# Folding two layer norms into the weights of a gated cross-attention block, with one norm chain and a reordered prologue

## The reference

```
# block 0: gated attention over the context, then RMS norm
memory_proj = context @ W_mem.T                     # (4, 512, 256)
attn        = softmax(x @ memory_proj.T / sqrt(256))
mc          = attn @ memory_proj
gate        = sigmoid(concat(x, mc) @ W_gate.T + b_gate)
fused       = x + gate * mc
x1          = fused * rsqrt(mean(fused^2) + 1e-6) * norm_w
# block 1: masked cross attention with 16 heads of 64, then a feed-forward part
q   = (layernorm(x1) * g_q + b_q) @ Wq / 8;  k, v = split(context @ Wkv)
x2  = x1 + tanh(attn_gate) * (softmax(where(mask, q @ k.T, -inf)) @ v) @ Wo
h   = gelu((layernorm(x2) * g_ff + b_ff) @ W1) @ W2
out = x2 + tanh(ff_gate) * h
```

## Time and profile before

| what | value |
|---|---|
| median of 3 executions | 231.49 us (231.4 to 231.99) |
| the profiled execution's own time | 232.58 us |
| its span, first to last instruction | 230.7 us |
| busy: PE, DVE, ACT, POOL | 212.7, 141.8, 127.4, 79.5 us |
| chain that ended last: PE, issue, DVE, POOL, ACT | 56%, 13%, 11%, 10%, 9% |

### The profile page before, as it was taken

One profiled execution on the slowest core, in us unless ns is written; L12 is line 12 of the kernel. 1 busy time (PEld: TensorE's weight loads), 2 busy tenths in 40 slices (PEclk: granted clock), 3 DMA queues, 4 the chain that ended last, 5 costly groups with the idle time before them and its releaser, 6 DMA issues.

```text
span 230.7 us, 4263 instructions
## 1 busy us (share of the span) xinstructions
PE 212.7 (92%) x1520; PEld 170.0 (74%) x1520; DVE 141.8 (61%) x296; ACT 127.4 (55%) x414; POOL 79.5 (34%) x82
## 2 busy tenths in 40 slices
PE   7769997998999999999999977999989999999994
PEld 4546544766976978976989855778867788998993
DVE  1575997635885556985655887867875567125410
ACT  3365754747457646567636466575449775028600
POOL 2030143943175333266331447636373007000000
PEclk9999997999999999999999999999999999999999
DMA  6984005050000000000000000050000000110011
GB/s 203 351 300 149 0 0 182 3 185 0 0 3 0 3 1 1 3 1 0 3 0 4 0 0 0 3 182 0 3 1 3 1 0 4 47 45 0 4 47 53
DMA packets 8463, 10.30 MB, mean 45 GB/s; under 512 B 754, under 2 KB 7668, under 8 KB 8052
## 3 DMA queue, kind: packets, MB, share of 16 engines
q1 hardware_dynamic: 7908, 9.71, 12.3%
q10 hardware_dynamic: 528, 0.26, 0.4%
HBM read 8.92 MB, written 1.05 MB: 43 GB/s over the span
## 4 chain that ended last, share of the span: by engine, by line
PE 56%; issue 13%; DVE 11%; POOL 10%; ACT 9%; POOLq 0%; ACTq 0%; DVEq 0%
PE bank L379 33%; ACT expd L585 6%; POOL probs L481 5%; PE bank L1080 4%; PE bank L1171 4%; PE bank L1050 3%; PE bank L1027 3%; PE bank L1090 3%; DVE neg_max L784 2%; PE bank L1229 2%; POOL wo_pair L519 1%; DVE probsT L797 1%; PE bank L1116 1%; PE bank L1134 1%; PE bank L1126 1%
## 5 line engine op out<-in xcount | busy, mean ns | idle before, releaser
L585 ACT ACTIVATE expd<-bank,neg_max 128x128 f32<-128x128 f32 (+1 forms) x136 | 50.5, 396 | 38.1 <-DVE neg_max L784 38.0
L481 POOL TENSOR_TENSOR probs<-expd,row_rcp 128x512 f32<-128x512 f32 x40 | 42.3, 1069 | 69.8 <-DVE row_rcp L792 63.2
L784 DVE TENSOR_REDUCE neg_max<-bank 128x4 f32<-128x512 f32 (+1 forms) x40 | 25.7, 683 | 6.0 <-PE bank L1050 3.6
L585 ACT ACTIVATION_READ_ACCUMULATOR expd<-bank,neg_max 128x1 f32 x136 | 29.3, 216 | 0.0
L379 PE MATMUL bank<-xhT_pair,wq_pair 128*128 128x256 f32 x192 | 27.5, 293 | 1.1 <-DVE fused L806 1.1
L379 PEld LDWEIGHTS bank<-xhT_pair,wq_pair 128*128 128x128 f32 x192 | 24.6, 194 | 5.0 <-DVE fused L806 1.9
L379 PE MATMUL bank<-wo_pair,oT_pair 128*128 128x256 f32 x192 | 26.6, 288 | 0.0
L1080 PE MATMUL bank<-ident,probs 128*128 128x128 f32 x160 | 22.6, 277 | 3.7 <-POOL probs L481 3.5
L379 PEld LDWEIGHTS bank<-wo_pair,oT_pair 128*128 128x128 f32 x192 | 23.6, 189 | 1.8
L1080 PEld LDWEIGHTS bank<-ident,probs 128*128 128x128 f32 x160 | 17.7, 140 | 8.4 <-POOL probs L481 7.1
L379 PE MATMUL bank<-wq_pair,gelu_pair 128*128 128x256 f32 x192 | 23.2, 281 | 0.4 <-issue 0.3
(11 more groups left out here) (125 smaller groups left out, 346.9 us busy)
## 6 DMA issues: line engine op xcount, KB each, us to landing
stage<-in_L_xattn_W_dram SPq DMA_DIRECT2D x2, 1024.0 KB, 5.0
x_sb<-in_x_dram SPq DMA_DIRECT2D x4, 256.0 KB, 8.7
wkv_sb<-in_L_xattn_Wkv_dram SPq DMA_DIRECT2D x1, 1024.0 KB, 9.2
stage<-in_L_xattn_Wq_dram SPq DMA_DIRECT2D x1, 1024.0 KB, 10.3
stage<-in_L_xattn_Wo_dram SPq DMA_DIRECT2D x1, 1024.0 KB, 5.4
out_dram<-x_sb SPq DMA_DIRECT2D x8, 128.0 KB, 1.7
ctx_sb<-in_ctx_dram SPq DMA_DIRECT2D x1, 768.0 KB, 7.1
probs<-in_L_xattn_W_gate_dram SPq DMA_DIRECT2D x1, 512.0 KB, 5.2
```

Source lines behind the costliest of these rows:

```text
L481: nc.gpsimd.tensor_tensor(probs[:, r, :].rearrange("p (h k) -> p h k", h=hb), expd[:, r, :].rearrange("p (h k) -> p h k", h=hb), row_rcp[: ...
L585: last = nc.scalar.activation(expd[:, r, h * w:(h + 1) * w], SC[n % 2][:, h * w:(h + 1) * w], ACT.Exp, bias=neg_max[:, r, h:h + 1], accum_ ...
L784: nc.vector.tensor_reduce(neg_max[:, r, 0:hb], SC[n % 2][:, :].rearrange("p (h k) -> p h k", h=hb), AX_X, ALU.max, negate=True).then_inc(d ...
```

## The change

- Both layer norms' scales are multiplied into Wq and W1 where these are split (a scale for each partition, since partition p holds rows 2p and 2p + 1). The offsets become biases of the queries and of the feed-forward part: `q_bias` and `f_bias`, 8 columns each, from 16 one-column float32 matmuls each (stages "qbias" and "fbias"). The query bias is added as queries are read from PSUM, the other one inside the Gelu. POOL's multiply and add on the normed tiles are gone.
- The chain of two norms becomes one. "rms" on DVE multiplies `fused` by the norm weight, takes statistics of that, then makes the mean square and var + epsilon x mean square; one power on POOL gives both roots. xhat comes from the product not yet scaled. POOL scales x_sb by the RMS root afterwards (in "xhat"). The stages "x1" and "ln1" are gone, and "xhat" stands where "x1" stood.
- A bank of keys is copied whole, odd ones by ACT and even ones by DVE.
- The prologue's order is new. Four broadcast rows of 128 KB are replaced by four loads of 2 values for each partition.

The diff, cut to its core (left out: allocations, semaphores, renamed views):

```diff
-    ("k", "hot", 0), ("splitq", 0), ("k", "hot", 3), ("gate", 0), ("k", "hot", 1), ("fuse", 0), ("rms", 0),
-    ("k", "hot", 2), ("k", "hot", 4), ("xT", 1), ("x1", 0), ("ln1", 0), ("k", "hot", 6), ("xhat", 0), ("k", "hot", 5),
-    ("y", 1), ("splitq", 1), ("k", "hot", 7), ("scores", "ctx", 1, 0), ("v", "hot", 0, 0), ("flag",), ("tiles",),
-    ("v", "hot", 1, 0), ("xhT", 0), ("v", "hot", 0, 1), ("norm", "ctx", 1, 0), ("exp", "ctx", 1, 0), ("q", 0, 0),
-    ("splito", 0), ("splito", 1), ("v", "hot", 1, 1),
+    ("k", "hot", 0), ("splitq", 0), ("k", "hot", 1), ("gate", 0), ("qbias",), ("k", "hot", 2), ("fuse", 0), ("rms", 0),
+    ("splitq", 1), ("k", "hot", 3), ("k", "hot", 4), ("xT", 1), ("xhat", 0), ("k", "hot", 5), ("tiles",),
+    ("y", 1), ("k", "hot", 6), ("xhT", 0), ("flag",), ("k", "hot", 7), ("scores", "ctx", 1, 0), ("q", 0, 0),
+    ("v", "hot", 0, 0), ("exp", "ctx", 1, 0), ("v", "hot", 0, 1), ("norm", "ctx", 1, 0),
+    ("splito", 0), ("splito", 1), ("v", "hot", 1, 0), ("v", "hot", 1, 1),
...
-    ((("x1", 1),), (("ln1", 1), ("q", 0, 3), ("xT", 2)), (("xhat", 1),)),
+    ((("xhat", 1),), (("q", 0, 3), ("xT", 2)), ()),
...
-    ((), (("gate", 1),), (("rms", 1), ("fuse", 1))),
-    ((("x1", 1),), (("q", 0, 3), ("ln1", 1)), (("xhat", 1),)),
+    ((), (("gate", 1),), (("rms", 1), ("fuse", 1), ("fbias", 0))),
+    ((("xhat", 1),), (("q", 0, 3),), ()),
...
-                    "xhT": [(dve["xhT"], c)], "k": [(dve["k"], c), (act["k"], c)],
+                    "xhT": [(dve["xhT"], c)], "k": [(act["k"], (c + 1) // 2)] if c % 2 else [(dve["k"], c // 2)],
...
+            for i, v in enumerate((lnq_g, lnq_b)):
+                load(lnq_cols[:, i, :], v.rearrange("(p k) -> p k", k=K), w_in["lnq"])
...
-            for i, v in enumerate((lnq_g, lnq_b, lnf_g, lnf_b)):
-                load(ln_rows[:, i, :], v.rearrange("(a d) -> a d", a=1).to_broadcast([P, D]), w_in["ln"])
+            for i, v in enumerate((lnf_g, lnf_b)):
+                load(lnf_cols[:, i, :], v.rearrange("(p k) -> p k", k=K), w_in["ln"])
...
+            sp.wait_ge(pe["qbias"], 1)
...
+            sp.wait_ge(pe["fbias"], 1)
...
-                        gp.wait_ge(dve["ms"], c)
-                        if c > 1:
-                            gp.wait_ge(dve["ve"], c - 1)
-                        nc.gpsimd.tensor_tensor(rms_r[:, :], ms[:, :], half_pow[:, :], ALU.pow
-                                                ).then_inc(pool["rms"], 1)
-                    elif st[0] == "ln1":
...
-                        nc.gpsimd.tensor_tensor(rstd[:, :], ve[:, :], half_pow[:, :], ALU.pow
+                            gp.wait_ge(pool["x1"], c - 1)
+                        nc.gpsimd.tensor_tensor(roots[:, :, :].rearrange("p a t -> p (a t)"),
+                                                squares[:, :, :].rearrange("p a t -> p (a t)"), half_pow[:, :], ALU.pow
...
-                    elif st[0] in ("xhat", "x2hat"):
-                        ln = 0 if st[0] == "xhat" else 2
-                        n = path.at[st] if ln == 0 else B + path.at[st]
-                        gp.wait_ge(dve[st[0]], c)
-                        if n == 1:
-                            gp.wait_ge(w_in["ln"], 64)
-                        normed = x2hat_buf(st[1]) if ln else xhat
-                        row = ln_rows[:, ln:ln + 2, :].rearrange("p (i a) d -> p i a d", a=1)
-                        nc.gpsimd.tensor_tensor(normed[:, :, :], normed[:, :, :], row[:, 0].to_broadcast([P, T, D]),
-                                                ALU.mult).then_inc(pool["scaled"], 1)
-                        gp.wait_ge(pool["scaled"], n)
-                        nc.gpsimd.tensor_tensor(normed[:, :, :], normed[:, :, :], row[:, 1].to_broadcast([P, T, D]),
-                                                ALU.add).then_inc(pool["affine"], 1)
+                    elif st[0] == "xhat":
+                        rows = x_sb[:, st[1] * T:(st[1] + 1) * T, :]
+                        gp.wait_ge(dve["xhat"], c)
+                        gp.wait_ge(pool["rstd"], c)
+                        nc.gpsimd.tensor_tensor(
+                            rows, rows, rms_r.rearrange("p (t a) -> p t a", a=1).to_broadcast([P, T, D]),
+                            ALU.mult).then_inc(pool["x1"], 1)
...
-                    elif kind == "ln1" and c == 1:
+                    elif kind == "rms" and c == 1:
...
-                    elif kind == "k":
+                    elif kind == "k" and c % 2:
...
-                            sc.wait_ge(act["k"], c - PAIRS)
-                        nc.scalar.copy(k_sb[0:DH, st[2], :, :],
-                                       path.bank(st)[0:DH, :].rearrange("p (s n) -> p s n", s=KT)
+                            sc.wait_ge(act["k"], (c - PAIRS + 1) // 2)
+                        nc.scalar.copy(k_sb[:, st[2], :, :], path.bank(st)[:, :].rearrange("p (s n) -> p s n", s=KT)
...
-                        nc.scalar.activation(wq_pair[:, HI, cols_of(st)], stage[:, cols_of(st)], ACT.Copy,
-                                             scale=DH ** -0.5).then_inc(act["wsplit"], 1)
+                        sc.wait_ge(dve["lnq"], 1)
+                        nc.scalar.activation(wq_pair[:, HI, cols_of(st)], stage[:, cols_of(st)], ACT.Identity,
+                                             scale=lnq_cols[:, 0, st[1]:st[1] + 1]).then_inc(act["wsplit"], 1)
...
-                        nc.scalar.copy(w1_parts[HI][:, cols_of(st)], stage[:, cols_of(st)]).then_inc(act["wsplit"], 1)
+                        sc.wait_ge(w_in["ln"], 32)
+                        nc.scalar.activation(w1_parts[HI][:, cols_of(st)], stage[:, cols_of(st)], ACT.Identity,
+                                             scale=lnf_cols[:, 0, st[1]:st[1] + 1]).then_inc(act["wsplit"], 1)
...
-                        nc.scalar.activation(expd[:, (c - 1) % RING, :], path.bank(st)[:, :], ACT.Gelu
-                                             ).then_inc(act["gelu"], 1)
+                        if c == 1:
+                            sc.wait_ge(dve["fbias"], 1)
+                        nc.scalar.activation(expd[:, (c - 1) % RING, :], path.bank(st)[:, :], ACT.Gelu,
+                                             bias=f_bias[:, m:m + 1]).then_inc(act["gelu"], 1)
...
+                        ve_.wait_ge(w_in["lnq"], 32)
+                        nc.vector.tensor_scalar(lnq_cols[:, :, :], lnq_cols[:, :, :], DH ** -0.5, None, ALU.mult
+                                                ).then_inc(dve["lnq"], 1)
+                    elif kind == "fbias":
+                        ve_.wait_ge(pe["fbias"], 1)
+                        nc.vector.tensor_copy(f_bias[:, :], path.bank(st)[:, 0:FM]).then_inc(dve["fbias"], 1)
+                    elif kind == "qbias":
+                        ve_.wait_ge(pe["qbias"], 1)
+                        nc.vector.tensor_copy(q_bias[:, :], path.bank(st)[:, 0:PAIRS]).then_inc(dve["qbias"], 1)
...
-                        ve_.wait_ge(act["square"], c)
-                        nc.vector.tensor_scalar(ms[:, :], sumsq[:, :], 1.0 / D, RMS_EPS, ALU.mult, ALU.add
-                                                ).then_inc(dve["ms"], 1)
-                    elif kind == "x1":
...
-                        ve_.wait_ge(pool["rms"], c)
...
+                        ve_.wait_ge(dve["gated"], T * c)
...
-                            last = nc.vector.scalar_tensor_tensor(
-                                x_sb[:, b * T + t, :], fused[:, t, :], rms_r[:, t:t + 1], normw_sb[:, :],
-                                ALU.mult, ALU.mult)
+                            last = nc.vector.tensor_tensor(x_sb[:, b * T + t, :], fused[:, t, :], normw_sb[:, :],
+                                                           ALU.mult)
...
-                    elif kind == "ln1":
...
-                        nc.vector.tensor_scalar(ve[:, :], mean_var[:, :, 1], LN_EPS, None, ALU.add
-                                                ).then_inc(dve["ve"], 1)
+                        ve_.wait_ge(act["square"], c)
+                        if c > 1:
+                            ve_.wait_ge(pool["rstd"], c - 1)
+                        chain(nc.vector.tensor_scalar(ms, sumsq[:, :], 1.0 / D, RMS_EPS, ALU.mult, ALU.add))
+                        nc.vector.scalar_tensor_tensor(ve, ms, LN_EPS, mean_var[:, :, 1], ALU.mult, ALU.add
+                                                       ).then_inc(dve["ve"], 1)
...
-                    elif kind == "k":
+                    elif kind == "k" and c % 2 == 0:
...
-                            ve_.wait_ge(dve["k"], c - PAIRS)
-                        nc.vector.tensor_copy(k_sb[DH:P, st[2], :, :],
-                                              path.bank(st)[DH:P, :].rearrange("p (s n) -> p s n", s=KT)
+                            ve_.wait_ge(dve["k"], (c - PAIRS) // 2)
+                        nc.vector.tensor_copy(k_sb[:, st[2], :, :],
+                                              path.bank(st)[:, :].rearrange("p (s n) -> p s n", s=KT)
...
```

(39 more changed lines are left out.)

41 lines of the change are left out of this document (23 added, 18 removed).

## The result

The changed kernel takes 246.62 us (median of 4 runs, 245.84 to 250.43) against 231.44 in the same comparison: ratio 1.0644, interval 1.0608 to 1.0679. The ratio leaves out the slow execution of 250.43 us (granted clock 0.959, against 0.972 to 0.986 in the others), so by the ratio it is 14.9 us slower, where +10.4 was forecast. The time lies at the upper end of the range (246.5): just inside it by the ratio (246.3), 0.1 above it by the median.

What follows compares the result with a forecast made beforehand. PE, busy 92% of the span, was taken to bound the kernel, other engines counting where PE waits. Prologue 5.0, batch 0 1.9, batch 1 2.5, batch 2 1.4 and tail -0.4 sum to +10.4 on 231.49: 241.9 us, range 235 to 246.5.

Steps and rivals of the forecast that it cites:

- rival C: Both bias groups: one-column matmuls cost 0.19 us a pair, prologue +2.9 more, batch 2 +1.5, total 246; chance 0.10.
- Rival A: Norm chain sets the pace; without POOL's two passes first head scores come before 41.99, total 228; chance 0.08.
- rival B: Whole kernel: gains and losses cancel, earlier idle times absorb both bias groups, total 231.5; chance 0.04.
- The pair price: Bias groups on PE: 0.10 us per weight load and matmul, 32 pairs, 3.2 us a group, bounds 1.8 and 3.5.
- Prologue: +5.0: Start to slot 1's scores: query-bias group, new waits and Wo's copies cost +5.0 us, bounds +3.5 and +7.9.
- Rival D: Clock falls behind PE's new idle stretches; one more loss than booked costs about 1.7 us, total 243.6; chance 0.18.
- Batch 0 +1.9: Slots 1 to 2: rms on DVE delays the query copy, scores +1.75; behind them no gain, 0.15 lost.
- batch 1 +2.5: Slots 1 to 2: the second norm's statistics already made the maximum late, so all 2.4 us of DVE delay count.
- Batch 2: +1.4: Feed-forward bias group and DVE's norm steps make the maximum 2.4 us later; slot 3 gains 1.0.
- (a): Batch 2: the 3.2 us bias group and DVE's 2.35 overlap, so the maximum comes 2.4 us later.
- (b): Batch 2, slot 3: without waits for POOL's passes it gains 1.0 us, bounds 0 and 2.6.
- Tail: -0.4: Batch 3 and tail: DVE's subtractions run less disturbed, -0.4 us, bounds 0 and -1.5; biased Gelu costs as before.

Runs made afterwards that it cites:

- e4: The kernel before, with POOL's scale and offset passes left out of both layer norms: 230.7 us, ratio 0.9994 to before.
- e5: The changed kernel with 128 moving columns instead of one in both bias groups, on the same weight loads: 246.14 us, 1.0629 of before.
- e1: The changed kernel run once more with no edit: 247.37 us, 1.0678 of before.
- e3: The changed kernel with query group 2's evacuation ahead of the rms steps in slot 1 of batches 0 and 1: 249.0 us, 1.0746 of before.
- e7: The changed kernel with the norm steps back at their old places in slot 2, the two roots still in one power: 246.75 us, 1.0616 of before.
- e2: The changed kernel with one of the 16 one-column matmuls in each bias group: 242.45 us, 1.047 of before.
- e6: The changed kernel with key 3, the flag and value (1,0) moved earlier in the prologue: 243.23 us, 1.0539 of before.
- e10: e9 with each one-column group cut to one of its 16 matmuls: 236.02 us, 1.0177 of before.
- e8: The kernel before, with whole key banks copied by one engine, odd by ACT and even by DVE: 231.45 us, 1.001 of before.
- e9: The changed kernel with the edits of e6 and e7 together: 242.32 us, 1.0489 of before.
- e12: e9 with the feed-forward bias group moved behind batch 3's xhat transposes: 241.4 us, 1.0411 of before.

## Why the prediction was right or wrong

**The measured time lies at the very end of the range, and not for the reasons that the range gave.** It was wide enough for a dearer pair (rival C), which did not come. What came is the lower clock in three places, 1.7, 1.6 and 1.5 us in single executions, where the sum has full speed; parts booked too high (batches 0 and 1, slot 1 of the prologue) took some of it back.

**Sign and place of the parts: right.** Prologue, slot 1 and batch 2 are where it was to come from, the squares were put at 29.2 (29.21), the transposes of xhat to end at 36.0 (start 35.59, 0.63 long), key 7 at 38.4 (38.26), the query copy in slot 1 nearly 3 us behind the output's (2.73), and the scores-to-probabilities time was to stay (4.21 and 4.25). Rival A, that the POOL passes set the pace, falls by its own sign (first head scores at 47.82, not before 41.99) and by e4, and rival B by the sum.

**The pair price** was 0.10 and is 0.109: +0.3 a group. The sentence of the Trainium skill that I put beside it (page "TensorE: Matmul & The Clock Gate", section "LDWEIGHTS (loading the stationary operand)": 107 ns for 128 columns) was nearer than my 0.10, and e5 shows that the moving columns don't set it. Rival C named the measured total (246), for a price of 0.19 a pair that no run shows: luck.

**Prologue: +5.0, measured +5.8.** The step that failed is "then key 7, context scores, queries and four values (7.7)". It took 9.56, because the flag wait that I had forecast (2.4, measured 2.03) brings the clock down behind it, and I priced the matmuls behind it at full speed. (Rival D says that one such loss stands on both sides. That of before is in its 41.99; the steps of the sum from 38.4 to 46.1 hold none.) The 1.8 us before the mask tiles did not appear: the lower clock behind the query-bias group stretched the key matmuls over it (that is argued from e5, where the wait is there, 1.58, and the clock up). And slot 1 did not wait for Wo's copies: +0.9 in my sum, 0.0 in e1.

**Batch 0 +1.9, measured +1.4; batch 1 +2.5, measured +1.6.** The mechanism is shown by e3 and e7, which both bring slot 1 to 2 back to 9.11. The sum has a slip of its own: its query copy ends at 61.6 against 59.63, which is +1.97 and not the +1.75 booked. And the size was off: rms takes 2.05 on DVE, not 2.35, and the scores follow the copy 0.74 behind instead of 0.99. That batch 1 pays for the second norm's statistics on top was wrong; they fit.

**Batch 2: +1.4, measured +5.4. This is the error of the forecast**, 4.0 of the 4.4 us that it was short. Two terms of it failed.

(a) "It and DVE's 2.35 overlap, they don't add: the max at 132.22 comes 2.4 later." That they overlap is true (e2). Over slots 1 and 2 e1 lost 4.0, and of that only 2.4 at full clock (e5). So 2.4 was the right number, but by luck: it is PE's group of 3.6 less 1.24 us of idle time that it fills, and not DVE's 2.35, for with the group cut the maximum is 1.9 late (e2). What the term lacked is the clock behind the group: transposes and head scores took 1.72 + 1.83 us where it had 1.04 + 1.05. That is most of the other 1.6.

(b) The 1.0 that slot 3 was to gain. It lost 1.4 in e1, and gained 0.1 in e6 (10.78), whose clock stayed up there: 1.5 of the error are the clock, 0.9 the gain that did not come. The POOL passes were hidden behind ACT's exps; the copy of the transposed xhat waits for these in any case (e10).

**Tail: -0.4, measured +0.5.** "The biased Gelu costs as before" is not so. Groups of after and of before:

```profile
L678 ACT ACTIVATE expd<-bank,f_bias 128x512 f32<-128x512 f32 x16 | 11.0, 688 | 6.0 <-PE bank L383 5.7
```

```profile
L675 ACT ACTIVATE expd<-bank 128x512 f32<-128x512 f32 x16 | 9.6, 599 | 6.9 <-PE bank L379 5.7
```

89 ns each, 1.4 us of ACT in all. The Trainium skill has it (page "ScalarE: Activation LUTs", section "What ACT_TABLE_LOAD costs": each per-partition pointer operand adds about 93 ns), and the trace agrees. That this is the 0.5 of the tail is argued; no run takes the bias out alone. The 0.5 are against the profile of before; the tails of e4 and e8, which compute the same Gelu without a bias, are 58.9 and 59.0, so the loss may be near 1.

**Rival D, the clock falls,** had the right mechanism and too small a size: 1.7 us in the prologue (e1 against e6), 1.6 behind the second group (e1 against e5), 1.5 to 1.6 in batch 2's slot 3 (e1 against e6, e10 against e9). Each is a difference of two single executions, and not all of them happen in each. That may be why e6 and e7 scatter by 3.6 and 5.1 us while e5, without the one-column stretches, scatters by 0.6. It is not shown: e12 has those stretches too and scatters by 0.9.

**What stays open:** why PE's idle stretches of 2 to 2.6 us in slot 3 lower the clock in some executions and not in others, why the clock falls within the group in some executions (3.9 to 4.6 us for it) and behind it in others, and what in POOL's multiply holds the small DVE instruction.

## What to carry to other kernels

Before work is folded away, ask what the kernel gains with that work simply left out: here nothing that could be measured (ratio 0.9994), on an engine with a third of its time busy. A bias by one-column matmuls costs the weight loads of full ones, here on the busiest engine. When two added pieces overlap, ask which idle time the longer one fills. And ask of every new idle stretch of PE, and of every stretch of one-column matmuls, what the matmuls behind it cost at the lower clock: here about 4.8 us in three places.

## What the runs showed of the hardware

- A float32 matmul on 128x128 weights costs 0.109 us a pair with one moving column and 0.112 with 128 (e1, e5).
- PE can lose its clock with no idle time ahead of it: behind 32 one-column pairs the granted clock is 0.62 (e1), behind 32 pairs of 128 columns 1.00 (e5). The Trainium skill says that the clock follows PE's recent activity (page "TensorE: Matmul & The Clock Gate", Part 1); the traces agree, and the prediction had left open what the one-column stretches do to it.
- A per-partition bias adds 89 ns to a Gelu of 512 columns (688 and 599 ns).
- A DVE instruction of 2 elements a partition with two tensor inputs took 0.16 us alone (e1) and 0.88 beside POOL's multiply of 128x512, ending when that ended; one with a single tensor input took 0.17 beside the same multiply (e9).
